# Gathers spaced by one filled word and four register steps, in place of three filled words

## The reference

```
e = stack([tbl_f[ids[:, f]] for f in range(32)], axis=1)      # (2048, 32, 64)
gram = einsum('bnd,bmd->bnm', e, e)
z = gram[:, rows, cols]              # the 496 pairs above the diagonal
h = concatenate([z, dense_ctx], axis=1)                       # (2048, 512)
h = maximum(h @ W_top1 + b_top1, 0)                           # 512 -> 512
h = maximum(h @ W_top2 + b_top2, 0)                           # 512 -> 256
y = h @ W_top3                                                # 256 -> 1
```

## Time and profile before

| | us |
|---|---|
| median of 3 runs | 421.49 |
| the 3 runs | 421.0, 421.49, 423.58 |
| the profiled execution's own time | 422.96 |
| its span, first to last instruction | 421.2 |
| mean granted TensorE clock (1.0 is full) | 0.992 |

### The profile page before, as it was taken

One profiled execution on the slowest core, in us unless ns is written; L12 is line 12 of the kernel. 1 busy time (PEld: TensorE's weight loads), 2 busy tenths in 40 slices (PEclk: granted clock), 3 DMA queues, 4 the chain that ended last, 5 costly groups with the idle time before them and its releaser, 6 DMA issues.

```text
span 421.2 us, 15063 instructions
## 1 busy us (share of the span) xinstructions
PE 383.8 (91%) x6516; PEld 214.8 (51%) x6516; DVE 229.9 (55%) x717; ACT 166.7 (40%) x264; POOL 276.7 (66%) x746
## 2 busy tenths in 40 slices
PE   0668777998989999999999999999999999989998
PEld 0334333555545555555446554555445555554576
DVE  2899999864647886017168886017158982000000
ACT  4346666522117835221444435221354425231222
POOL 7888888864446888565588998565588888410000
PEclk9999999999989999999999999999999999998999
DMA  5944841210003786100187622100177111015610
GB/s 162 381 143 138 261 165 42 47 42 18 19 17 62 142 206 209 20 19 16 31 161 163 192 67 49 19 20 17 23 143 166 37 21 23 16 29 105 121 52 0
DMA packets 38236, 37.51 MB, mean 89 GB/s; under 512 B 13781, under 2 KB 26903, under 8 KB 38042
## 3 DMA queue, kind: packets, MB, share of 16 engines
q1 hardware_dynamic: 29546, 28.54, 26.6%
q0 software_dynamic: 6144, 6.30, 7.2%
q10 hardware_dynamic: 2480, 1.71, 1.5%
HBM read 28.45 MB, written 8.09 MB: 87 GB/s over the span
## 4 chain that ended last, share of the span: by engine, by line
PE 76%; DVE 15%; ACT 3%; DMA 3%; issue 2%; ACTq 1%; DVEq 0%
PE sel_ps L522 37%; PE tower_ps L568 13%; DVE onehot L467 11%; PE gram_ps L553 10%; PE tower_ps L578 6%; PE gat_ps L522 3%; PE gat_ps L538 3%; PE tower_ps L522 3%; DVE tabs L455 2%; DVE work L450 2%; ACT vecs L333 2%; PE tower_ps L587 1%; DMA ids_wide<-ids_scratch 1%; DMA ids_scratch<-sel_f 1%; ACTq L181 1%
## 5 line engine op out<-in xcount | busy, mean ns | idle before, releaser
L467 DVE TENSOR_SCALAR onehot<-ids_wide,row_ids 128x512 bf16<-128x512 f16 x688 | 201.3, 364 | 101.0 <-PE sel_ps L522 86.4
L296 POOL DMA_INDIRECT rows<-in_tbl_dram,gat_ids x192 | 195.8, 1020 | 74.0 <-PE gram_ps L553 55.5
L522 PE MATMUL sel_ps<-onehot,tabs 128*64 128x512 bf16 x1872 | 211.7, 382 | 30.0 <-DVE onehot L467 17.7
L522 PEld LDWEIGHTS sel_ps<-onehot,tabs 128*64 128x64 bf16 x1872 | 110.6, 110 | 126.0 <-issue 30.0
L333 ACT COPY vecs<-sel_ps 64x256 f32<-64x256 f32 x144 | 87.2, 606 | 95.4 <-PE sel_ps L522 75.8
L292 POOL MEMSET spare<- 128x1 f32 x546 | 80.7, 148 | 20.4
L568 PE MATMUL tower_ps<-work,w_sb 128*128 128x512 f32 (+1 forms) x160 | 58.7, 515 | 0.2 <-ACT h L356 0.2
L553 PEld LDWEIGHTS gram_ps<-vecs 64*32 64x32 f32 x4096 | 38.4, 105 | 25.4 <-issue 25.3
L553 PE MATMUL gram_ps<-vecs 64*32 64x32 f32 x4096 | 42.5, 201 | 4.4 <-issue 4.3
L568 PEld LDWEIGHTS tower_ps<-work,w_sb 128*128 128x128 f32 x160 | 29.2, 190 | 20.9 <-issue 18.5
L474 DVE COPY work<-gram_ps 128x512 f32<-128x512 f32 x8 | 5.2, 685 | 54.6 <-PE gram_ps L553 54.6
(11 more groups left out here) (19 smaller groups left out, 64.4 us busy)
## 6 DMA issues: line engine op xcount, KB each, us to landing
ids_wide<-ids_scratch SPq DMA_DIRECT2D x40, 256.0 KB, 6.6
rows<-in_tbl_dram,gat_ids POOLq DMA_INDIRECT x192, 2.5
products<-work SPq DMA_DIRECT2D x12, 248.0 KB
products<-work SPq DMA_DIRECT2D x24, 120.0 KB
work<-in_packed_dram SPq DMA_DIRECT2D x5, 512.0 KB, 5.7
work<-products SPq DMA_DIRECT2D x9, 256.0 KB, 4.5
work<-in_packed_dram SPq DMA_DIRECT2D x3, 640.0 KB, 5.3
work<-in_packed_dram ACTq DMA_DIRECT2D x2, 512.0 KB, 4.4
```

What stands on the lines that cost most here:

```text
L296: nc.gpsimd.indirect_dma_start(out=rows[:, r, k, h, :], out_offset=None, in_=tables[GATHERED[k]], in_offset=bass.IndirectOffsetOnAxis(ap=g ...
L467: last = nc.vector.tensor_scalar(onehot[:, n % RING, c - c0, :], ids_wide[:, k, :], row_ids[chunks[k]][:, c:c + 1], None, ALU.is_equal)
L522: last[at] = nc.tensor.matmul(sel_bank(u, g)[DIM * at:DIM * at + DIM, :], tabs[:, first_chunk[k] + c, part, :], onehot[:, piece_no(u, g, h ...
```

## The change

Behind each gather there is now one fill, then a wait of POOL's queue for that fill, and then a number of additions to a register `pause`: four, or none behind the gathers 48 to 62. No instruction uses the register's value. The wait for the fill, which stood ahead of the next fill and never ahead of a gather, now stands ahead of the first addition or, where there is none, ahead of the next gather.

```diff
-NEAR_SPACERS, SPACERS = 1, 3
+NEAR_STEPS, STEPS = 0, 4
 NEAR_SPACED = range(48, 63)
...
             count = itertools.count()
 
-            def spacer():
-                n = next(count)
-                if n > 0:
-                    pool.wait_ge(spaced, n)
+            pause = pool.alloc_register("pause")
+            pool.reg_mov(pause, 0)
+
+            def space(steps):
+
                 nc.gpsimd.memset(spare[:], 0.0).then_inc(spaced, 1)
+                pool.wait_ge(spaced, next(count) + 1)
+                for _ in range(steps):
+                    pool.reg_add(pause, pause, 1)
...
                     gather(u, r, x, k, h)
-                    for _ in range(NEAR_SPACERS if len(of_unit) * u + n in NEAR_SPACED else SPACERS):
-                        spacer()
+                    space(NEAR_STEPS if len(of_unit) * u + n in NEAR_SPACED else STEPS)
```

## The result

The median went from 422.29 us (15 runs) to 424.80 us (15 runs). The ratio is 1.0059, with a 95% interval of 1.0040 to 1.0077: slower by about 0.6%, or 2.5 us. That is less than the 1% which the prediction took as the least that can be told from no change, but with 15 runs of each the interval leaves out 1: in us it is 1.7 to 3.3.

The account below looks back on a forecast made before the run. PE was taken as the bound, with DVE setting the pace in unit 0 up to 68 us. Added DVE losses of 2.1 us there and 0.1 in units 1 to 3 gave +2.2: 421.49 to 423.7 us, range 419.5 to 427.5.

Parts of the forecast that it names:

- The steps are worth nothing: POOL's register additions behind each fill: taken as worth almost nothing, since no instruction reads the register and they may be dropped.
- Two fills fewer cost DVE nothing: POOL's 364 or so removed fills: counted at 0.00 for DVE, with at most 0.7 us to gain.
- The rival of fills that hold DVE: Fills beside one-hots cost DVE 0.10 us each, so removing them gains 4 us: 417.5 us, chance 0.05.
- A gap of 0.14 + 0.28 = 0.42 us: POOL, gather's end to next start: one fill of 0.14 plus a wait of 0.28, in place of 0.71 or 0.58.
- A second loss in a half-pair: Unit 0: two slow one-hots of DVE per half-pair in place of one, 14 x 0.147 = 2.1 us more.
- 0.1 us at the three places in units 1 to 3: Where DVE's ten one-hots are late for PE: more frequent gathers add 3 x 0.3 x 0.147 = 0.1 us.
- The chain leaves DVE at 70 in place of 68 us: Marker in unit 0: the chain of waits was to go from DVE to PE at 70 us, not 68.
- The range: Time of the likeliest case, 423.7 us: 420.5 to 427; with the same-step case and its spread, 419.5 to 427.5.
- Same step (421.5 us): Executed steps make the gap 0.54 to 0.62 us, every loss stays where it was: 421.5 us, chance 0.26.
- Steps that stop the queue (455 us): Executed steps delay the next gather's preparation, gap 1.12 us, POOL becomes the bound: 440 to 470, say 455, chance 0.17.

Follow-up runs that it names:

- steps_alive: The changed kernel with its four register steps kept in the program (add 1, remainder by 7, twice): median 485.0 us, ratio 1.1496 to the kernel before.
- two_fills: The kernel before with two fills behind a gather in place of three and no wait ahead of a gather: ratio 1.0075 to the kernel before.
- two_waited: The changed kernel with two fills behind a gather, each waited for (one behind gathers 48 to 62), and no register: ratio 1.0011 to the kernel before.
- unit0_old: Unit 0 spaced as in the kernel before (three fills), units 1 to 3 as in the changed kernel: ratio 0.9999 to the kernel before.
- one_event: The changed kernel with no-operations in place of the register steps, built as one EVENT_SEMAPHORE behind each fill: 433.7 us against 421.75 in one run.
- anchored: The kernel before with unit 0's gathers 5 to 21 placed by a semaphore of DVE, one fill behind gathers 26 to 47: ratio 0.9988.

## Why the prediction came out right

The forecast of 423.7 us was 2.2 above the median that was known; measured were 2.5 above. That the two are within 0.3 us is in part luck: the interval spans 1.6 us, and of the 2.2 the traces bear out the 1.7 in unit 0.

- **The steps are worth nothing.** Right, and more plainly than I had put it: they aren't in the program. What steps cost that are in it, steps_alive shows.
- **Two fills fewer cost DVE nothing.** Right; the number removed is 546 - 192 = 354, not 364. two_fills and two_waited have the same 369 fills, and their ratios differ by 0.6%; after has 192 and two_fills 369, and their mean one-hots are within 2 ns. The rival of fills that hold DVE falls.
- **A gap of 0.14 + 0.28 = 0.42 us.** Right: 0.15 + 0.27. The 0.14 was luckier than it looks: it is a third of a row of 0.43 that also holds the pauses between three fills of 0.10 to 0.12, while a fill beside one-hots takes 0.15. Where the fill is short, beside a subtraction, it is 0.11 + 0.27 = 0.38.
- **A second loss in a half-pair.** Right, in mechanism and size: the half-pair is 3.51 us long against 3.38 + 0.15 = 3.53. Forecast were 14 more losses and 2.1 us up to 68 us; there are 12 more, 1.75 us: I had taken the second loss for each of the 14 half-pairs of eight one-hots, and two went without it (those ahead of the subtractions at 14.04 and 22.06). The two half-pairs of ten had two losses each before, as taken, and have two after. The mean one-hot was forecast at 375 ns and is 374.
- **0.1 us at the three places in units 1 to 3.** Wrong in sign, and without weight. PE's idle time at the three transitions summed to 2.01 us in before and 1.53 in after; the ten one-hots of the first (the earlier trace rows has 3.13) take 2.89:

```profile
141.23 2.89 DVE onehot L470 x10
```

  unit0_old has the short gap there and its ratio is 0.9999. How many gathers fall on those three stretches of 2.9 us is chance, and I had made a mean of it.
- **The chain leaves DVE at 70 in place of 68 us.** The subtraction that it named is at 69.82, but the chain itself reads otherwise, since PE was at half clock there and DVE waited for it. The chain of waits of after:

```profile
61.30 1.41 DVE work L453
...
66.47 5.16 PE sel_ps L525 x30
...
71.70 3.03 DVE onehot L470 x10
```

  The 30 matmuls that took 3.43 us in the earlier trace rows take 5.16. Such a marker should be an instruction of the engine, not the place where the chain changes engines.
- **The range.** Its upper end doesn't follow from its terms: 421.5 + 2.2 + 0.5 + 1 is 425.2, not 427. The measured 424.80 lies inside either.
- **Same step (421.5 us).** Didn't happen, but its reasoning is true: a gap below 0.71 can give the same step, as two_waited shows with 0.54 and 0.68.
- **Steps that stop the queue (455 us).** Its gap of 1.12 us is what steps_alive has (1.11 to 1.14), and its 0.42 + 0.50 = 0.92 is what one_event has. The price was too low for the first: 485. The lateness of the rows was priced nearly right: 8 to 25 us in unit 0 and 8.5 in each of the others, 34 to 50 in all, against waits of PE of 22.3 us and then 9.3, 10.6 and 8.8, 51 in all. In unit 0 each half-pair let only one gather through, so that 19 in place of 33 left from 11.5 to 71 us. What the price left out are the 12.5 us by which PE's matmuls take longer, at a lower mean clock. The Trainium skill (Perfetto Trace Analysis, § Sequencer-only Instruction) says that the next instruction is decoded only when the sequencer is done with such an instruction; the 0.72 us from the last step to the gather agree with it, though no run shows what they consist of.

## What to carry to other kernels

Where two engines disturb each other only at the end of an instruction, what counts is where those ends fall, so a "cheaper" filler that shortens a gap can cost time on the engine beside it; read a half-cycle of both timelines instruction by instruction, and ask on which instruction the next end will land. Look whether an added instruction is in the built program before costing it, and where it might be there, price the case of it too: here it was the difference between 0.6% and 15%. And compare medians, not the spans of two profiles, when the effect is no larger than one stretch of half clock.

## What the runs showed of the hardware that I had not expected

- **A wait of its own ahead of a gather costs 0.5 us of latency.** In after a gather that must wait for a fill and for PE has two waits, and the one for PE stands ahead as an EVENT_SEMAPHORE. The chunk at 183.80 ends at 185.09, and the gather starts 0.78 us after that, not 0.28 as in the earlier trace rows:

```profile
183.80 1.29 PE L556 MATMUL gram_ps<-vecs 64*32 64x32 f32 x128
...
185.87 0.94 POOL L300 DMA_INDIRECT rows<-in_tbl_dram,gat_ids  x1 [2.46 <-PE gram_ps L556]
```

  All 27 gathers that wait for a chunk start 0.720 to 0.731 us after such an instruction. In the prediction this rested on a single row and its fellow. Where such an instruction finds its wait satisfied (13 waits for a transpose), it costs nothing: the gather starts 0.21 after it, and 0.27 behind the fill like the others. Off the critical path, as here, the 0.5 us are free (unit0_old).
- **Register steps.** Those that ran took 35 to 40 ns each and started 0.07 us apart, and they expose the 0.72 us even though they wait for nothing themselves but the first.
- **A gather that outlasts a subtraction ends 0.82 us behind it.** A gather beside no subtraction takes 0.94 to 1.14 us. One that overlaps a subtraction of DVE by more than 0.05 us and doesn't end inside one ends 0.81 to 0.83 us behind the subtraction's end, whenever it started: so it is in all 158 such cases in the ten profiles. The one at 39.70 in before started 0.94 us into the subtraction and takes 1.09; the one at 40.01 in after, 0.38 into it, takes 1.65; those of unit 0 in steps_alive, 0.2 ahead of it, take 2.24; the one at 24.33 in anchored, 0.70 ahead, takes 2.73. What holds a gather back there no run shows.
